# Small multiplies placed between the routers' scatters on GpSimd

## The reference

```python
top2 = jnp.argmax(logits_no1, axis=-1)
loc1 = jnp.cumsum(m1, axis=0) - 1.0
loc2 = jnp.cumsum(m2, axis=0) - 1.0 + m1.sum(axis=0, keepdims=True)
m1 = m1 * (loc1 < C)
m2 = m2 * (loc2 < C)
dispatch = d1 + d2
xin = jnp.einsum('tec,td->ecd', dispatch, xt)
h = jnp.einsum('ecd,edf->ecf', xin, fc1_w) + fc1_b[:, None, :]
```

## Time and profile before

| what | value |
|---|---|
| time, median of 3 runs | 1337.3 us |
| the three runs | 1335.68, 1337.3, 1352.05 us |
| profiled execution, its own time | 1334.83 us |
| its span (first to last instruction) | 1332.8 us |
| PE busy | 1086.0 us, 81% |
| DVE busy | 697.6 us, 52% |
| ACT busy | 604.3 us, 45% |
| POOL busy | 480.1 us, 36% |
| granted TensorE clock, mean | 0.885 |

### The profile page before, as it was taken

How to read it: one execution, slowest core, us unless ns; L and a number is a source line. 1 busy time by engine, 2 the same in 40 slices (tenths; PEclk the granted TensorE clock), 3 DMA queues, 4 the chain that set the end, 5 groups by cost and what they waited for, 6 DMA issues and landing times. The chain is left out here.

```text
span 1332.8 us, 26518 instructions
## 1 busy us (share of the span) xinstructions
PE 1086.0 (81%) x8602; PEld 751.1 (56%) x8602; DVE 697.6 (52%) x3341; ACT 604.3 (45%) x1521; POOL 480.1 (36%) x728
## 2 busy tenths in 40 slices
PE   6999777799949999989896866985777999962884
PEld 4777554477815666664343753985643444541673
DVE  7666463233358776645364631112757888755002
ACT  3544544433249766634222421432462666631553
POOL 4767433243317555522004444343020000066243
PEclk9999897799969999999997975998685999975887
DMA  8789600122059950010740022664041212005433
GB/s 232 235 224 174 182 25 24 56 87 86 16 107 136 175 104 1 1 45 24 149 94 1 2 92 66 173 173 140 2 142 32 69 57 69 28 21 160 130 104 100
DMA packets 141767, 124.60 MB, mean 93 GB/s; under 512 B 13919, under 2 KB 116737, under 8 KB 141641
## 3 DMA queue, kind: packets, MB, share of 16 engines
q1 hardware_dynamic: 130488, 106.77, 34.2%
q0 software_dynamic: 7168, 12.83, 3.0%
q10 hardware_dynamic: 3984, 3.42, 0.8%
HBM read 88.12 MB, written 37.70 MB: 94 GB/s over the span
## 5 line engine op out<-in xcount | busy, mean ns | idle before, releaser
L955 ACT ACTIVATE L_Z<-L_Z,L_nmx 128x154 f32<-128x154 f32 x256 | 105.2, 414 | 43.3 <-DVE L_nmx L1002 43.1
L3476 DVE CUSTOM_DVE_ANT_0 L3s_masked<-L3s_psS,L3s_trilw 128x512 f32<-128x512 f32 (+3 forms) x256 | 109.8, 487 | 24.0 <-PE L3s_psS L3303 23.5
L325 POOL TENSOR_TENSOR L_Z<-L_Z,L_mx 128x512 f32<-128x512 f32 x84 | 87.4, 1041 | 65.2 <-DVE L_mx L700 63.3
L3431 ACT ACTIVATE L3s_E<-L3s_psT 128x512 f32<-128x512 f32 (+1 forms) x192 | 87.7, 530 | 49.4 <-PE L3s_psT L3316 49.2
L846 POOL TENSOR_TENSOR L_Z<-L_Z,L_rin 128x488 f32<-128x488 f32 x64 | 64.0, 1000 | 102.0 <-DVE L_rin L1010 102.0
L871 PE MATMUL L_psS<-L1k_G,L_xnT 128*128 128x462 f32 x192 | 83.7, 533 | 2.7 <-DVE L_nmx L1002 1.3
L700 DVE CUSTOM_DVE_ANT_0 L_Z<-L_psS,L_Z 128x154 f32<-128x154 f32 x256 | 63.5, 315 | 32.6 <-PE L_psS L381 30.0
L1002 DVE CUSTOM_DVE_ANT_0 L_Z<-L_psS,L_mask 128x154 f32<-128x154 f32 x256 | 67.9, 314 | 11.9 <-PE L_psS L871 11.2
L556 ACT ACTIVATE L_E<-L_psT 128x512 f32<-128x512 f32 x84 | 46.1, 596 | 52.0 <-PE L_psT L394 50.9
L1020 DVE COPY L_PT<-L_psT 122x512 f32<-122x512 f32 x64 | 43.7, 683 | 40.2 <-PE L_psT L881 39.3
L3303 PE MATMUL L3s_psS<-L3s_KS,L3s_QS 72*128 72x512 bf16 (+3 forms) x256 | 55.4, 333 | 7.5 <-PEq L3289 4.6
(11 more groups left out here) (626 smaller groups left out, 2829.0 us busy)
## 6 DMA issues: line engine op xcount, KB each, us to landing
L_Z<-in_fside_Bx16xSxS SPq DMA_DIRECT2D x16, 1232.0 KB, 7.3
L2f_w<-in_L_ffn_W SPq DMA_DIRECT2D x39, 256.0 KB
slotsL<-empty SPq DMA_DIRECT2D x1, 8320.5 KB, 67.0
L1m_cb<-comb_rows SPq DMA_DIRECT2D x8, 1024.0 KB, 10.1
L3f_w<-in_L_ffn_fc_w SPq DMA_DIRECT2D x32, 256.0 KB
L0f_w<-in_L_ffn_W SPq DMA_DIRECT2D x24, 256.0 KB
L3s_QS<-q_parts SPq DMA_DIRECT2D x144, 32.0 KB
L3s_KS<-k_parts SPq DMA_DIRECT2D x48, 96.0 KB
```

The costliest lines, as they stand in the source:

```text
L325: nc.gpsimd.tensor_tensor(Z[:, t % NZ, h, 0:KM_], Z[:, t % NZ, h, 0:KM_], top.broadcast_to([P, HG, KM_]), ALU.subtract).then_inc(z_ready, 1)
L955: last = nc.scalar.activation(Z[:, t % 2, h], Z[:, t % 2, h], ACT.Exp, scale=-1.0, bias=nmx[:, t % 2, h:h + 1], accum_out=sums[:, t % 2, h ...
L3431: nc.scalar.activation(E[:, g.par, h, EO[group[0]]:EO[group[0]] + wd], psT[:, k, 0:wd], ACT.Exp).then_inc(t_free, 1)
L3476: last = nc.vector.tensor_tensor_reduce(masked[:, k, at:at + wd], psS[:, k, at:at + wd], trilw[:, S - wd:S], 1.0, LOW, ALU.add, ALU.max, m ...
```

## The change

Each router gets a tile `pause` of 128x12 and a counter of the scatters sent. After the second, fourth and sixth scatter of every chunk of eight, GpSimd multiplies a column of ones with a column of ones and writes it to a column of `pause` of its own. Nothing reads `pause`, and the multiply has no wait and sets no semaphore. There are 12 per router and 36 in the program.

```diff
@@ -1465,6 +1465,7 @@
             self.both = ctx_tile("both", [P, TB, E], BF)
+        self.pause, self.sent_rows = sb("pause", [P, 12]), 0
         self.own = sem("route_own")
@@ -1722,6 +1723,10 @@
     def send_one(self, pool, slots, k, t, landed):
         pool.indirect_dma_start(slots, bass.IndirectOffsetOnAxis(ap=self.m.slot_to[:, k, t:t + 1], axis=0), self.pay[:, k, t], None,
                                 bounds_check=slots.shape[0] - 1, oob_is_err=False).then_inc(landed, 16)
+        self.sent_rows += 1
+        if self.sent_rows % 8 in (2, 4, 6):
+            n = self.sent_rows // 8 * 3 + self.sent_rows % 8 // 2 - 1
+            self.nc.gpsimd.tensor_tensor(self.pause[:, n:n + 1], self.m.ones[:, 0:1], self.m.ones[:, 0:1], ALU.mult)
```

## The result

| | before | with the change |
|---|---|---|
| time, median of 20 runs each | 1339.34 us (1325.87 to 1352.05) | 1347.91 us (1336.9 to 1356.04) |
| profiled execution | 1334.83 us | 1339.1 us |
| its span | 1332.8 us | 1337.3 us |
| granted TensorE clock, mean | 0.885 | 0.878 |
| POOL busy | 480.1 us | 488.2 us |

The ratio on record is 1.0056, with a 95% interval from 1.0035 to 1.0078: 7.5 us slower, where 1.3 us were forecast. (It is not the quotient of the two medians, which differ by 8.6 us.) The time is above the range of 1334.5 to 1343.2 us.

What follows compares the result with a forecast made beforehand. Waits for GpSimd's scatters and layer 3's barrier were taken to bound it. Twelve multiplies on the path at 0.11 us made 1.3 us, the others nothing: 1337.3 + 1.3 = 1338.6 us, range 1334.5 to 1343.2 us.

Steps and rivals of the forecast that it cites:

- What bounds the kernel: Step: TensorE waits for `xs` loads issued after all scatters; GpSimd ends layer 3's barrier last, by 2.7 us.
- twelve places on the path: Last chunks of layers 0 and 2, chunks 0 and 3 of layer 3: three multiplies each, 1.3 us together.
- The price of one multiply: Step: a multiply between two GpSimd scatters lengthens the pair by 0.11 us, range 0 to 0.44 us.
- not hidden: Denies a rival: free GpSimd cores or the scatter gap swallow the multiply; price 0, time 1337.3 us, chance 0.13.
- the queue does not break: Denies a rival: every multiply pays the empty-queue price, 0.44 us; 5.9 us in sum, 1343.2 us, chance 0.12.
- The sum, place by place: Step: of 36 multiplies only twelve, before waits that end last, count; 12 x 0.11 = 1.3 us.
- Chunk 1 is covered by 3.89 us: Layer 3: GpSimd's idle time before chunk 2, waiting for `slot_to`, hides chunk 1's multiplies; cost 0.
- chunk 2 by 0.68 us: Layer 3: chunk 3 started 0.68 us later than it could have, hiding chunk 2's shift of 0.33 us; cost 0.
- layer 2's chunks 1 and 2 by 4.13 us: Idle time before layer 2's last chunk hides six multiplies of 0.66 us; cost 0.
- where I had 0.66: Layer 3's forecast cost: 0.33 us for chunk 0 before the barrier and 0.33 us for chunk 3 before the `xs` wait.
- The held scatter: Rival, layer 3: shifted order brings a second hold by VectorE, 1.96 us; sum 3.3 us, 1340.6 us, chance 0.05.
- The clock: Rival: TensorE's clock rises at other times in three expert stages, about 6 us either way, 1332 to 1345 us; chance 0.1.

Runs made afterwards that it cites:

- e5: Kernel before plus four multiplies at each of the 12 places forecast to be on the path, none elsewhere; ratio to before 1.0048 (1.0017 to 1.0078), long chip.
- e15: Repeat on a short chip: four multiplies at each of the 12 path places, none elsewhere; ratio to before 1.0041 (1.0015 to 1.0067).
- e17: The change, without an edit, measured again on a long chip; ratio to before 1.0021 (0.9991 to 1.0051).
- e1: The change with the tile `pause` kept and all 36 multiplies left out, short chip; ratio to before 0.9974 (0.9952 to 0.9996).
- e12: Repeat of the tile `pause` alone, all 36 multiplies left out, short chip; ratio to before 1.0005 (0.9980 to 1.0030).
- e10: The change, without an edit, measured a third time, on a short chip; ratio to before 1.0002 (0.9981 to 1.0022).
- e9: The kernel before, unchanged, measured as if it were a change, short chip; ratio to before 0.9996 (0.9973 to 1.0018).
- e2: The change, without an edit, measured again on a short chip; ratio to before 1.0041 (1.0012 to 1.0071).
- e13: The change, without an edit, first of two on one short chip; ratio to before 1.0016 (0.9991 to 1.0041).
- e14: The change, without an edit, second of two on one short chip; ratio to before 1.0035 (1.0009 to 1.0062).
- e19: Kernel before plus three multiplies at each of 18 covered places, none on the path, long chip; ratio to before 0.9904 (0.9870 to 0.9938).

## Why the prediction was wrong

- **What bounds the kernel**: right in its two points, the wait for the scatters and the barrier, where GpSimd is last in every trace. e5 and e15 agree with twelve places on the path: 6.4 and 5.4 us where their sum is 6.2.
- **The price of one multiply**: right. 0.11 us forecast, 0.10 measured; it is not hidden, and the queue does not break.
- **The sum, place by place** is the step that failed: its terms for the multiplies in front of a wait for `slot_to`, which it put at nothing. "Chunk 1 is covered by 3.89 us", chunk 2 by 0.68 us and layer 2's chunks 1 and 2 by 4.13 us were idle times of one execution on one long chip, and the 3.89 us held a late start of 3.69 us. On the short chips these waits don't exist. The six multiplies at nothing in layer 3 cost one scatter more behind the hold, and the layer 0.3 + 1.5 = 1.8 us, where I had 0.66. Layer 2 costs 1.1 and layer 0 0.5 us or more, where I had 0.33 each.
- On the long chip of the first profile the waits did exist. In layer 2 they covered, with 2.86 us left of 4.13. In layer 3 they moved: from 4.86 us in sum to 6.33 us, and 2.33 us in e17. There the cover is real but its size is not the kernel's own, it holds late starts.
- The sum becomes 0.5 + 1.1 + 1.8 = 3.4 us on the short chips, a ratio of 1.0026. That lies inside 1.0028 +- 0.0020, the mean of six measurements, and near 1.0023, the mean of the four on short chips. That layer 2's 1.1 us arrive at the end of the kernel is not shown: from its chunk 1 to layer 3's chunk 0 it is 388.6 to 391.8 us in before and e1 and e12, and 390.3 to 391.2 us with the change. Without these 1.1 us the sum would be 2.3 us, inside too.
- **The held scatter** was a rival at 2.0 us with a chance of 0.05. On the short chips it came true in a form that I had not thought of: no second hold, but the one hold fell on the scatter ahead, so that one more of 1.28 us stands behind it. My argument against it looked for a multiply inside the hold. The place of the hold among the scatters was what moved.
- **The clock** as a rival: it was told apart by dose. If it enlarged small delays several times, four multiplies a place would have cost 10 us and more. The profiled clock of 0.878 against 0.885 is not shown to come from the multiplies: a profile of the change on a short chip, e10, has 0.892, against 0.889 of before in e9. Over all runs of a set the change's mean clock is never above before's, and lower by 0.003 in e2 (0.889 against 0.892) and by 0.0001 to 0.0014 in e10, e13, e14 and e17; of before beside the first result no clocks are on record. A loss by the clock that does not grow with the delay is not ruled out by these runs.
- **The range** took its width from the costs of the change, 8.7 us, around a median of three runs, 1337.3 us. Twenty runs of before gave 1339.34 us, so 2.0 us of the miss lie in the starting point. What is left, the 7.5 us of the first ratio against the 3.8 us of the mean, is not explained by a cause that I could show, and stays open; a deviation of 0.3% in such a ratio is as large as most of its intervals here. A range that allowed for it, 4 us on each side, would have reached 1347 us, still 0.7 us short of the time. That the time lies above the range is thus in part the wrong terms, in part the starting point, and in part unexplained.

## What to carry to other kernels

A wait that covers added work has to be asked what ends it. When somewhere in the chain that ends it a start is marked as remote, or lies microseconds behind the end of the instruction that should release it, it may be gone on another chip, and the added work then lies on the path. So read a second profile, of another chip if there is one, before a cover goes into a sum. Before a small effect is explained, make it large: four multiplies a place stood clear of zero in both measurements, one multiply in three of six. And where an engine's memory instruction can be held by another engine's long one, count the instructions that will stand behind the hold after the shift: work ahead of it costs nothing until the hold falls on another instruction, and then a whole one.

## What the runs showed of the hardware

- Further multiplies behind the first cost less than the first does: four take 0.64 us together and lengthen the pair by 0.52 us, where one takes 0.22 and lengthens it by 0.10 us (the four write bf16, the one float32). The page GPSIMD Engine Reference of the Trainium skill, section 2.1, says that consecutive GpSimd instructions are no barrier between its cores; four at 0.64 us, 0.14 us for each after the first, agree with an overlap of neighbours, though no run tells it from a fixed start cost.
- A scatter that starts while VectorE's instruction of 2.35 us, with two SBUF inputs, runs is held until that one is done: 1192.16 + 2.16 = 1194.32 us in e9, 0.85 us behind the end of that instruction at 1191.12 + 2.35 = 1193.47; and 1197.22 + 2.64 = 1199.86 us in e10, 0.84 us behind its end at 1199.02. In all 20 profiles the held scatter ends 0.84 or 0.85 us behind that instruction, while its own length runs from 2.16 to 2.93 us. That agrees with the lock that the Trainium skill (SBUF — State Buffer, section on two separate sides) describes, and it gives the price of this hold: the scatter ends 0.85 us behind VectorE, however early it began.
- Chips differ by 31 to 35 us in this kernel, 1306 against 1337 to 1341 us, and the waits differ with them. Among the 200 largest groups of waits, none is marked as remote in any of the eleven profiles of short chips; in each of the nine of long chips there are four to nine such groups, with 20.3 us (e19) to 59.6 us (before) of idle time in sum. Not all of it is on the path, and what ends these waits is not known. An example: ScalarE's copy of a TensorE result in layer 0 starts 9.3 us behind the end of the transposes in the first profile (195.50 + 0.63 = 196.13 us, the copy at 205.43 us), with the release marked as remote. In e9, on a short one, it follows 0.03 us behind them (197.26 + 0.63 = 197.89 us, the copy at 197.92 us).
- The kernel's spread from run to run, 18 us on one chip, goes with the granted clock: of the 29 runs of before beside e1, the six with the lowest mean clock (0.885 to 0.889) have spans of 1304.5 to 1310.8 us, the eight with the highest (0.895 to 0.899) 1292.7 to 1303.7 us. Which of the two makes the other, these runs don't tell.
